# Second attention layer: value products of two key tiles in a row, and earlier products of the query weights

## The reference, cut to what matters

```python
# layer 0: queries over a compressed width of 96, 16 heads of 128, plus rotary parts of 64
q_c = q @ W_dq                      # 1024 x 96
q_nope = q_c @ W_uq                 # 16 heads x 128
k_nope = (kv @ W_kvc) @ W_uk
...
# layer 1: 16 heads of 16, 1601 keys for each batch
q = _qdq(x) @ _qdq(wq).T + bq
kv = cond @ wkv.T + bkv
attn = jax.nn.softmax(jnp.einsum('bnhd,bmhd->bhnm', q, k) * scale, axis=-1)
o = jnp.einsum('bhnm,bmhd->bnhd', attn, v).reshape(B, N, C)
out = _qdq(o) @ _qdq(wp).T + bp
```

## Time and profile before

| | |
|---|---|
| median of three runs | 819.45 us |
| profiled execution, its own time | 820.73 us |
| its span in the trace | 818.9 us |
| PE busy | 757.7 us, 93% |
| DVE busy | 565.7 us, 69% |
| ACT busy | 383.9 us, 47% |
| POOL busy | 197.3 us, 24% |
| first and last `scores` of the second layer | start at 371.75 us, and at 793.88 us |

### The profile page before, as it was taken

One profiled execution on the slowest core, in us unless ns is written; L12 is line 12 of the kernel. 1 busy time (PEld: TensorE's weight loads), 2 busy tenths in 40 slices (PEclk: granted clock), 3 DMA queues, 4 the chain that ended last, 5 costly groups with the idle time before them and its releaser, 6 DMA issues.

```text
span 818.9 us, 13086 instructions
## 1 busy us (share of the span) xinstructions
PE 757.7 (93%) x5026; PEld 428.6 (52%) x5027; DVE 565.7 (69%) x1290; ACT 383.9 (47%) x562; POOL 197.3 (24%) x208
## 2 busy tenths in 40 slices
PE   7999999977989989879999999999999999899996
PEld 3545767753745655644444454654455554345434
DVE  4687989531446566597787878777787777897814
ACT  2100443443423223216666657466666566574670
POOL 2298313220930131110220402300505001300000
PEclk9799999999999999999999999999999999999999
DMA  9200000205298330445055282550380820560000
GB/s 302 124 0 1 1 1 1 81 0 184 72 132 146 104 49 20 49 58 88 2 116 67 81 152 31 120 75 2 142 121 15 143 39 1 107 76 14 2 1 14
DMA packets 32476, 55.94 MB, mean 68 GB/s; under 512 B 11572, under 2 KB 20532, under 8 KB 31509
## 3 DMA queue, kind: packets, MB, share of 16 engines
q1 hardware_dynamic: 32408, 55.04, 33.5%
HBM read 42.56 MB, written 12.46 MB: 67 GB/s over the span
## 4 chain that ended last, share of the span: by engine, by line
PE 68%; DVE 18%; issue 6%; POOL 4%; ACT 2%; DMA 1%; SPq 0%; DVEq 0%; POOLq 0%; ACTq 0%
PE ps L1096 12%; PE ps L985 12%; PE ps L1075 9%; PE ps L873 5%; DVE small L1656 5%; PE ps L883 3%; PE ps L752 3%; PE ps L949 3%; PE ps L929 3%; PE ps L799 2%; PE ps L842 2%; PE ps L759 2%; PE ps L830 2%; DVE small L1606 1%; PE ps L1057 1%
## 5 line engine op out<-in xcount | busy, mean ns | idle before, releaser
L1656 DVE TENSOR_REDUCE small<-ps 128x1 f32<-128x400 f32 (+1 forms) x512 | 285.9, 572 | 83.1 <-PE ps L985 77.0
L1467 ACT ACTIVATE r<-ps 128x1024 f32<-128x1024 f32 (+1 forms) x208 | 212.6, 1024 | 90.4 <-PE ps L1075 87.7
L985 PE MATMUL ps<-r 96*128 96x400 bf16 (+1 forms) x512 | 171.3, 342 | 14.6 <-DVE small L1656 12.1
L1096 PE MATMUL ps<-r 128*17 128x256 f32 (+1 forms) x1664 | 131.2, 387 | 2.3 <-ACT r L1467 2.0
L1075 PE MATMUL ps<-r 99*128 99x256 bf16 (+1 forms) x832 | 126.5, 274 | 0.0
L985 PEld LDWEIGHTS ps<-r 96*128 96x128 bf16 x512 | 49.6, 97 | 127.3 <-DVE small L1656 93.4
L1075 PEld LDWEIGHTS ps<-r 99*128 99x128 bf16 (+1 forms) x832 | 81.6, 100 | 31.7 <-issue 9.5
L633 POOL TENSOR_TENSOR r<-r 128x400 bf16<-128x400 f32 (+1 forms) x32 | 29.4, 951 | 202.4 <-ACT r L1308 202.4
L929 PE MATMUL ps<-r,hT 128*128 128x512 f32 (+1 forms) x160 | 69.1, 564 | 0.0
L873 PE MATMUL ps<-r,wkvT 128*128 128x400 f32 (+1 forms) x128 | 53.4, 516 | 5.5 <-issue 5.5
L883 PE MATMUL ps<-wkvT,r 128*128 128x256 f32 (+1 forms) x208 | 55.5, 383 | 0.0
(11 more groups left out here) (201 smaller groups left out, 1028.4 us busy)
## 6 DMA issues: line engine op xcount, KB each, us to landing
r<-kscr SPq DMA_DIRECT2D x96, 200.1 KB, 8.8
kscr<-r SPq DMA_DIRECT2D x24, 400.2 KB, 3.8
r<-in_ctx_dram SPq DMA_DIRECT2D x4, 1601.0 KB, 7.0
r<-qscr SPq DMA_DIRECT2D x24, 128.0 KB, 5.0
r<-in_wo_dram SPq DMA_DIRECT2D x1, 2048.0 KB, 12.0
r<-in_gu_dram SPq DMA_DIRECT2D x1, 2048.0 KB, 7.7
qscr<-qpart SPq DMA_DIRECT2D x24, 64.0 KB, 1.7
x<-in_x_dram SPq DMA_DIRECT2D x1, 1024.0 KB, 5.3
```

The source lines that it names most:

```text
L985: mm(bank(ca % 2)[:, 0:m], qst[0:SROWS, h, q0:q0 + P], kst[0:SROWS, s % 2, h % HALF, a:a + m], start=True, stop=True).then_inc(mx_mm, 1)
L1096: last = mm(bank(6)[32 * k:32 * k + VW, 0:LQ], vx[0:n, b % 2, kt, h, :], pr[i % 3][0:n, k * LQ:(k + 1) * LQ], start=kt == 0, stop=kt == KT ...
L1467: fn(pr[i % 3][0:n, :], bank(2 + 2 * (i % 2), 2)[0:n, :], ACT.Exp, scale=SCALE1)\
L1656: v.tensor_reduce(mxc[quad % 2][:, n:n + 1], bank(ca % 2)[:, 0:m], AX_X, ALU.max).then_inc(mx_rdy, 1)
```

## The change

`weighed(quad, kt)` says which steps are weighed in a step: in every even step from 2 on the two steps before it (two calls of `weigh` in a row, 16 records), in step 0 the last step of the quad before, and in odd steps none. `step_work` and `chunk_room`, from which the chunks of maxima get their places, count the columns of `weigh` by that.

At the start of the first layer, the 16 products of the query weights move in between the turned tiles, four each behind tiles 3, 4, 5 and 6; the first half of the projection of the queries stands behind tile 5's. ACT copies them in the same order.

```diff
-        work = [chunk_room(beside.get((i // KT, i % KT), [])) for i in window]
+        work = [chunk_room(beside.get((i // KT, i % KT), []), i % KT) for i in window]
...
+def weighed(quad, kt):
+    i = KT * quad + kt
+    if kt == 0:
+        return [i - 1] if quad else []
+    return [i - 2, i - 1] if kt % 2 == 0 and quad < QUADS else []
...
-    return 4 * LQ + 4 * LQ + sum(cost.get(kind(j), 0) for j in jobs)
+    return 4 * LQ + 4 * LQ * len(weighed(1, kt)) + sum(cost.get(kind(j), 0) for j in jobs)
...
+            def query_down(hf):
+                pe.wait_ge(xnT_ev, 4 * hf + 4)
+                for c in range(FC):
+                    last = mm(bank(4 - hf)[0:QC, :], wdq[:, c, :], xnT[:, c, hf * 512:(hf + 1) * 512], start=c == 0,
+                              stop=c == FC - 1)
+                last.then_inc(qc_mm, 1)
...
                 last.then_inc(xnT_mm, 1)
-
-            pe.wait_ge(ld_q, 96)
-            for h in range(H):
-                last = mm(bank(h // 8)[0:QC, (h % 8) * KVC:(h % 8 + 1) * KVC], wuq[:, h, :], wuk[:, h, :],
-                          start=True, stop=True)
-                if h % 8 == 7:
-                    last.then_inc(m_mm, 1)
...
+                if t == 3:
+                    pe.wait_ge(ld_q, 96)
+                if t >= 3 and t < 7:
+                    for h in range(4 * (t - 3), 4 * (t - 3) + 4):
+                        last = mm(bank(h // 8)[0:QC, (h % 8) * KVC:(h % 8 + 1) * KVC], wuq[:, h, :], wuk[:, h, :],
+                                  start=True, stop=True)
+                        if h % 8 == 7:
+                            last.then_inc(m_mm, 1)
+                if t == 5:
+                    query_down(0)
+            query_down(1)
...
-                        if quad or kt:
-                            weigh(KT * quad + kt - 1)
-                        pace(4 * LQ)
+                        for i in weighed(quad, kt):
+                            weigh(i)
+                        pace(4 * LQ * len(weighed(quad, kt)))
...
+                if t == 5:
+                    act.wait_ge(ld_q, 96)
+                    weights_made(0)
+                elif t == 6:
+                    query_down(0)
+            weights_made(1)
+            query_down(1)
```

More of the change, by code:

```diff
@@ L119, in tail_bank, with step_work, chunk_room @@
     return 7 if b + 1 < B else {"turn_x": 5, "up": 0, "gate": 1, "down": 2, "expert": 3}.get(part, 7)
-def step_work(jobs):
+def weighed(quad, kt):
[3 more added lines that the diff above has]
+    return [i - 2, i - 1] if kt % 2 == 0 and quad < QUADS else []
+def step_work(jobs, kt):
     cost = {"k": 8 * 401, "v": 16 * D, "out": 2 * 4 * P, "shift": 8 * P, "up": 16 * D, "down": 16 * D,
             "expert": 16 * D, "turn_x": 4 * 4 * P, "turn_o": 4 * P, "project": 4 * D, "gate": 4 * 4 * E}
-    return 4 * LQ + 4 * LQ + sum(cost.get(kind(j), 0) for j in jobs)
-def chunk_room(jobs):
+    return 4 * LQ + 4 * LQ * len(weighed(1, kt)) + sum(cost.get(kind(j), 0) for j in jobs)
+def chunk_room(jobs, kt):
     busy = {"out": 2 * 2 * D, "bias": 2 * 2 * D, "scale": 3 * 2 * D, "round": 4 * 2 * D, "project": 2 * 2 * D,
@@ L133, in chunk_room @@
             "gate": 2 * 2 * D, "down": 3 * 2 * D, "expert": 2 * 2 * D}
-    return max(0, step_work(jobs) + 1969 - 0.6 * sum(busy.get(kind(j), 0) for j in jobs))
+    return max(0, step_work(jobs, kt) + 1969 - 0.6 * sum(busy.get(kind(j), 0) for j in jobs))
 def first_chunks(t, third):
@@ L1212, in _ @@
                     others = [j for j in jobs if j[0] != "max"]
-                    total, count = step_work(others), len(maxima)
+                    total, count = step_work(others, kt), len(maxima)
                     passed = [0]
@@ L1248, in _, with weights_made, query_down @@
             fn(kvtok, bank(5)[:, 0:B * KVC].rearrange("p (b n) -> p b n", b=B), ACT.Copy).then_inc(kvt_ev, 1)
+            def weights_made(g):
+                act.wait_ge(m_mm, g + 1)
+                src = bank(g)[0:QC, :].rearrange("p (h n) -> p h n", h=8)
+                fn(weff[:, 8 * g:8 * g + 8:2, R:P], src[:, 0::2, :], ACT.Copy)
+                fn(weff[:, 8 * g + 1:8 * g + 8:2, 0:KVC], src[:, 1::2, :], ACT.Copy).then_inc(m_ev, 1)
+            def query_down(hf):
+                act.wait_ge(qc_mm, hf + 1)
+                fn(qcT[:, hf * 512:(hf + 1) * 512], bank(4 - hf)[0:QC, :], ACT.Copy).then_inc(qc_ev, 1)
             for t in range(TILES):
```

## The result

| | before | after |
|---|---|---|
| median (lowest to highest) | 819.86 us (819.33 to 822.75) | 840.12 us (838.57 to 841.6) |
| ratio to before, 95% interval | | 1.0236 (1.0213 to 1.0258) |
| profiled execution, span | 820.73, 818.9 us | 840.29, 838.5 us |
| first `scores` of the second layer | 371.75 us | 367.46 us |
| first to last `scores` | 422.13 us | 446.10 us |

A forecast was written before the change was run, and what follows sets the result against it. PE's order of products was taken to bound the second layer's steps, DVE second. 820.73 - 17.8 + 19.5 + 12 - 1.3 = 833.1 us, forecast at 832 as the median lies 1.3 lower; range 814 to 843, the forecast's own 825 to 840.

The forecast's parts named there:

- Part 1: Second layer's value blocks, two in a row: 0.20 us saved at each of 89 double blocks, 17.8 us in all.
- Rival B: Double blocks: second block's weights load with the array idle, 0.10 us each, half the saving goes; 841 us, chance 0.09.
- Rival D: Double blocks save nothing while waits come, both ways in and out being paid inside; 850 us, chance 0.03.
- Part 2: Chunks between double blocks: PE waits for reduced chunks, 23.9 us against 4.4 before, so 19.5 us added.
- Both rules: Chunk banks: free 1.01 us after the chunk's start; for a chunk next to another, 1.50 after the first's start.
- the remaining 40 wait for nothing: 40 of 96 pieces between double blocks: no chunk waits, as a projection or tail product of 0.4 us or more intervenes.
- the upper bound of 30 us: Most that added chunk waits could reach, if DVE's other work in these steps falls on each of them.
- Part 3: Shift after the split of the maxima: it loses cover and waits longer, about 12 us added (ends 5 and 17).
- the 2 us of remaining waits: Shift: of 3.65 us of earlier waits left beside the four long ones, 2 were given to the other 11 quads.
- Part 4: First layer's start: products moved between the turned tiles save 1.3 us (nothing to 3).
- A: Added waits at chunks and shift cover each other, half of 31.5 us come, kernel gets faster; 816 us, chance 0.22.
- C: Gains and waits cancel, DVE's split being hidden elsewhere; 820 us, chance 0.07.

The follow-up runs named there:

- the first experiment: Only the first layer's start changed against the kernel before, with its value blocks and chunks as before: 815.75 us against 820.51, ratio 0.9937.
- the planned double blocks: Kernel after the change, with chunk places and 60 double blocks set by a searched table: 803.02 us, ratio 0.9784 to the kernel before.

## Why the prediction was right

The forecast of 832 us had the sign and the mechanism; the time was 8 us longer, inside the range of 814 to 843 but 0.12 us above the forecast's own range of 825 to 840. That it came so near is in part luck: 7.7 us more were saved than forecast and 15.0 us more lost, and of the latter the larger part in things that the sum had at nothing. Point by point, in the terms of its sum for the profiled execution (833.1 us forecast, 840.29 measured):

**Part 1, 17.8 us saved: 22.5.** The double block takes 0.99 us to the next chunk where I had 1.02. 72 of the 96 do so; others are stretched by waits that count as excess. The last quad, where I had given the blocks nothing, got 1.1 us shorter. Rival B, the second block's weights loaded with the array idle, is refuted by that 0.99: it would have needed 1.12 or more. So of the two statements of the Trainium skill (TensorE: Matmul & The Clock Gate; the narrow one, that a load overlaps products in flight only where the row group differs, stands in Part 3 under The mechanism, not under the heading that the prediction names, and the wider one in Part 2, Step-by-step: what each phase is for) the trace speaks against the narrow one, between two blocks too: all these products use the same rows of the array. That it is the background buffer which hides the load, no run here shows. Rival D falls with the same number.

**Part 2, 19.5 us of waits for chunks: 16.7, and 12.8 us beside them.** The excess outside the shift steps grew by 29.5 us: 13.1 bare, 12.7 with other work, 3.7 the rest. Both rules hold to the hundredth: third chunk 1.01 us after the first, fourth 1.49 after it, and a bare pair takes 3.19 us (583.01 to 586.20; I said 3.2, before it was 2.88).

To see how much of the 29.5 are waits for chunks, I took from the two traces all chunks outside the shift steps that start within 0.11 us of the end of the reduction that frees their bank, and added up how much later they start than such a chunk does elsewhere. That is worked out, like the table. It gives 9.0 us before and 25.7 after. Behind reductions alone it is 3.7 and 21.7 us, where my two rules gave 4.4 and 23.9. So this term of the sum had the right mechanism and about the right size. One step of it failed by a little: "the remaining 40 wait for nothing". In steps with products of other work the chunks are late by 4.4 us (before 2.0).

The other work of DVE, which I had given as the reason for the upper bound of 30 us, holds up chunks for 4.1 us, less than before (5.3), so it is no part of the growth. Where it does, it costs much. PE and DVE in such a step:

```profile
609.84 1.06 PE L1109 MATMUL ps<-r 128*17 128x256 f32 x16
610.83 0.52 PE L998 MATMUL ps<-r 96*128 96x401 bf16 x2
...
611.91 0.34 PE L998 MATMUL ps<-r 96*128 96x400 bf16 x1 [0.34 <-DVE small L1677]
...
613.17 0.34 PE L998 MATMUL ps<-r 96*128 96x400 bf16 x1 [0.70 <-DVE small L1677]
...
611.28 0.57 DVE L1677 TENSOR_REDUCE small<-ps 128x1 f32<-128x401 f32 x1 [0.72 <-PE ps L998]
611.77 0.74 DVE L1783 TENSOR_SCALAR r<-r,small 128x256 f32<-128x256 f32 x2
612.54 1.59 DVE L1677 TENSOR_REDUCE small<-ps 128x1 f32<-128x400 f32 x3
```

The second chunk's reduction has to stand behind L1783, the scaling of the tail, and the fourth chunk comes 2.34 us after the first instead of 1.49. This happens in quads 4, 8 and 12, 0.86 us each.

The largest term that the sum lacked is in the jobs of other work. The prediction says "the chunks alone change steps, no DMA and no job does", and costs them at nothing. It is true that none changes its step, but in an odd step no block stands between the four scores and the job any more. The job comes sooner and finds bank 7, which the jobs share, not yet read. PE in step 5 of quad 7, where `keys` (L886) follows the scores, and the instruction of ACT that reads bank 7 for the job before:

```profile
580.05 0.60 PE L1088 MATMUL ps<-r 99*128 99x256 bf16 x4
581.04 0.94 PE L886 MATMUL ps<-r,wkvT 128*128 128x400 f32 x2 [0.39 <-ACT r L1329]
...
580.40 0.59 ACT L1329 ACTIVATE r<-ps,bk 128x400 bf16<-128x400 f32 x1
```

The product starts 0.99 us after the scores, where 0.44 are enough. From start to start the products of the jobs are late by some 7 us after and by 1 before, so 6 of the 29.5 us are this. Another 2 are the clock's: outside the shift steps PE ran at 0.50 for 10.96 us after and for 6.83 before, most of it in the step behind a shift. The last 5 us are spread over many small distances; what causes them is open.

**Part 3, 12 us at the shift: 17.0.** The four long waits were forecast at 2.4 to 2.9 us each, 10.4 in all. Measured are 3.22, 2.90, 2.90 and 1.33 idle us before `shift` in quads 3, 7, 11 and 13, 10.35 (before 5.65, two of them at a chunk). That the sum agrees is luck: the first is above what I had given and the last about half of it, and that one isn't for the split at all but for bank 7 (L1842). The other 11 quads idle 0.81 to 1.38 us each, 11.1 in all, where they idled 0.6 before: 10.5 more, and I had 9.7. The step that failed is the 2 us of remaining waits that I took off: they were not at these shifts. The rest of the 17.0 is 1.8 us. The clock can be no more than 0.8 of it: only 1.5 us at 0.50 lie in shift steps and outside a wait; the remaining 1.0 is open. The prediction had left the clock out of the sum, at 3.4 us for all steps, and it came about so: PE's clock stood at 0.50 from 469.9, 596.2 and 719.1 us on, 13.65 us in all against 6.83 before, some 3 us of time. The quad that has it first, from the windows, answers to the earlier trace rows:

```profile
469.90:476.70 6.80, 5.64 (x35) 2.67 (x35) 3.52 (x7) 2.04 (x2) 0.99 (x2) 0.50 0.46 181
```

**Part 4, 1.3 us saved: 4.3** (4.1 in the first experiment). The products moved as I said, but the step that failed is that I held PE's clock at 0.50 until nearly the same time. In the trace after the tiles and the products between them run at the full clock, and the first product for the heads starts at 28.19 us instead of 33.23:

```profile
18.91 0.81 PE L747 MATMUL ps<-r 128*96 128x64 f32 x8
19.85 0.44 PE L740 MATMUL ps<-ident,xn 128*128 128x128 f32 x2
...
21.98 1.91 PE L731 MATMUL ps<-r 128*96 128x512 f32 x4
...
25.46 1.96 PE L731 MATMUL ps<-r 128*96 128x512 f32 x4 [0.47 <-ACT r L1274]
28.19 1.95 PE L765 MATMUL ps<-r 96*128 96x512 f32 x4 [0.78 <-ACT r L1270]
```

Eight records of the short products take 0.81 us here, where 32 took 5.28 before, four long ones 1.91 where eight took 5.42.

**The other rivals.** A (half of the waits, 816 us) needed DVE to catch up while PE waits. It is the other way round: DVE starves for 0.82 us in the double block and PE then waits for four reductions. A's price was right in one respect, the order can be made such that the waits stay away (803.02 us), but not this order. C (820 us) falls with the visible 0.81 at every ordinary shift.

The terms together: 3.0 us more saved at the start and 4.7 in the blocks, 15.0 more excess, 7.3 us above the sum.

## What to carry to other kernels

When an engine's work is bunched, price what the bunch starves before pricing what it saves: here 0.23 us saved in a bare pair with four chunks cost 0.5 us of waits, because two banks and a ring of 1.01 us can't store the work of 1.0 us. Lay the rules along every stretch and for every shared buffer, not only for the one that the change is about: jobs that keep their step can still come sooner inside it, and here that cost 6 us at bank 7. Look, too, for what stood between the last producer and a short serial chain such as the split: that cover has no instruction of its own in the diff, and its loss cost more (17.0 us) than the bare steps together (13.1).

## What the runs showed of the hardware

**Short DVE instructions beside POOL.** The instructions of the split other than the reduction end about when a POOL instruction ends (in quad 3 within 0.04 us): the first takes 0.53 and the others 0.85 to 0.87 us in quad 3, where POOL's follow each other every 0.90, and 0.17 or 0.18 where POOL is idle. The reduction over the same buffer, L1680, takes 0.19 in both. The Trainium skill (SBUF — State Buffer, Who interferes with whom) says that DVE instructions in a two-port mode hold a port pair shared with GpSimd for the whole instruction, that those with two inputs from SBUF contend with GpSimd instructions that read SBUF, and that a reduction on this chip never does. The trace agrees for L1685 and L1688, which have two inputs, and for the reduction; in which mode L1684 and the cast L1687 ran, no row shows. The three waits of 3.22, 2.90 and 2.90 us stand where POOL works beside the split.

**PE's clock at the start.** In both profiled kernels with the old start the clock stood at 0.50 for 13.65 us from 16.8 or 17.0 us on. In the eight with the early part (this change and seven experiments) it did so for 3.41 us at most in the first 31 us, and in three of them not at all. Why it fell at 17.0 us isn't shown by this: the products that were moved stand behind the fourth tile's, which starts at 16.90 before, so up to there the order of PE is the same. In one experiment with the early part (the planned double blocks) it fell as well, at 18.27, and was back after 3.41 us. What the moved products may explain is thus how long the clock stayed down, and not that it fell. PE's busy time alone doesn't decide that either: before, PE was in work without a pause from 22 to 30 us, and the clock stayed at 0.50.

**PE's clock in the steps.** In the ten traces PE waited 18 times for more than 1.5 us in the second layer's steps. At 15 of these waits the clock fell to 0.50, in the wait or within 1.7 us of its end, and stood there for 3.41 or 6.83 us; the three others (1.63, 1.71 and 2.81 us) had no such fall. Two stretches at 0.50 had no such wait ahead of them. So a long wait usually costs 1.7 or 3.4 us more than itself, but not always.
